# A new order of the steps of all five engines in a fused cross-attention and feed-forward kernel on one core

## Chip, cores, metric

The kernel runs on one NeuronCore of a Trainium2 chip (trn2). The metric is the device time of one execution in microseconds (us), median of the runs. The engines are TensorE (PE), VectorE (DVE), ScalarE (ACT), GpSimd (POOL) and SyncE (SP), which issues the DMA transfers. Each engine takes its instructions in order; between engines the program waits on semaphores.

## The reference

Eight batches of 512 rows with D = 512 go through cross-attention to 120 keys with 16 heads of 32, and then through a feed-forward block of width F = 2048 whose inputs are rounded to 8 bits and whose weights are rounded to three values. Cut to what matters:

```python
q = layernorm(x);  Q = q @ wq + bq;  K = ctx @ wk + bk;  V = ctx @ wv + bv
s = where(mask == 0, 1e-9, einsum('bhqd,bhkd->bhqk', Q, K) / sqrt(32))
x = x + (softmax(s) @ V) @ wo + bo
def bitlinear(x, w, b):                     # act_quant: round to 127 / max|x|; weight_quant: to -1, 0, 1
    return einsum('bsd,fd->bsf', act_quant(rmsnorm(x)), weight_quant(w)) + b
h = gelu(bitlinear(layernorm(x), w1, b1))
x = x + bitlinear(h, w2, b2)
```

## The kernel before

The 4096 rows are 32 tiles of 128 rows, numbered k = 0 to 31, four to a batch. A tile passes through a chain of steps, each a small helper that waits on semaphores, issues a few instructions on one engine and counts a semaphore up:

- layernorm by batch: SP `load_x` (L362, one 1 MB load of a batch), DVE `ln1_stats` (L1491), POOL `ln1_apply` (L2117), PE `turn_xn` (L535, transposes; the fourth of a batch lets SP load the next batch), ACT and DVE evacuate a high and a low part;
- attention: PE `project_q` (L528 in the helper `product3`, twelve matmuls: high and low parts), `project_ctx` (L560), `scores` (L581); DVE `softmax_max` (L1505, L1508), ACT `exps` (L1089), DVE `invert_sums` (L1513), POOL `normalize` (L2161), PE `turn_probs` (L591), ACT `evac_probs` (L1061), PE `attend` (L603), DVE `oT_low` (L1470), PE `project_out` (L528 again), DVE `residual` (L1518). `normalize`, `turn_probs` and `exps` go by quarter tiles, n = 4k to 4k + 3;
- first rounding: DVE `ln2_stats`, `ln2_scales` (L1524 to L1541), POOL `round_x` (L2129, L2134), then SP `turn_x(k)` (L328), a DMA transpose of the rounded tile q_x into `q_xT`. It waits for `round_x(k)` and for PE's use of an older buffer;
- feed-forward: PE `ffn_up(k, c)` for four chunks c (L632; chunk 0 waits for `q_xT`), DVE `evac_up` (L1554), ACT `gelu` (L1096), `square_h` (L1130), DVE `h_scale` (L1562), POOL `round_h` (L2172, L2177), SP `turn_h(k)` (L337), a DMA transpose of q_h into `q_hT` four times as large as that of q_x, PE `ffn_down(k, half)` for two halves (L655; the first waits for `q_hT`), POOL `h_factor` (L2195 to L2204) and `add_b2` (L2156), DVE `evac_down` (L1574), SP `store(k)` (L354). `load_residual(k)` (L323) brings the tile of x that the residual needs into one of six buffers and waits until the store of tile k - 6 has landed. ACT needs a table load when it changes between exponentials and gelu.

What sets the order is written out by hand: for each engine one list of calls in its block function (SP from about L369, PE from about L690, ACT from about L1156, DVE from about L1646, POOL from about L2217). Each list has a first part (the weights are loaded, transposed and rounded, the pipeline fills), `for a in range(2, 6)`, and a last part. One pass of the loop is one batch: four tiles in each step, several tiles deep, so that `scores(4a)`, `project_out(4a - 2)`, `ffn_up(4a - 4, 2)` and `ffn_down(4a - 5, 0)` stand near each other. SP's list in the loop begins with `store(4a - 6)`; all its transfers go through one queue in the order of issue:

```python
turn_x(4 * a - 2)
turn_h(4 * a - 4)
load_x(a + 2)
```

For the last tiles some steps go to other buffers: near the end `ffn_up` also writes banks that belonged to attention (`ps_s`, `ps_t`; DVE evacuates into `wk_s`, `wv_s`), the last tile is rounded in halves, and SP's `turn_last` brings the halves of it to PE.

Of the kernel before, what the change touches and what calls it, by code (L numbers as in the profile page):

```python
# [27 lines left out]
def xattn_bitffn_kernel(nc, x, ctx_in, mask, wq, bq, wk, bk, wv, bv, wo, bo, w1, b1, w2, b2, out):  # L28
# [104 lines left out]
    with ExitStack() as stack:  # L133
# [170 lines left out]
        def _(sp):  # L304
# [86 lines left out]
            load_piece(6)  # L391
            load_piece(5)
            load_residual(0)
            load_residual(1)
            load_piece(7)
            load_x(2)
            load_residual(2)
            load_residual(3)
            load_mask(1)
            load_ctx(2)  # L400
            load_residual(4)
            turn_x(0)
            load_residual(5)
            turn_x(1)
# [3 lines left out]
            store(0)  # L408
            turn_x(3)
            turn_h(1)  # L410
            load_mask(2)
            load_residual(6)
            turn_h(2)
            load_ctx(3)
            store(1)
            turn_x(4)
            load_residual(7)
            turn_h(3)

            for a in range(2, 6):  # L420
                store(4 * a - 6)
                turn_x(4 * a - 3)
                load_residual(4 * a)
                turn_x(4 * a - 2)
                turn_h(4 * a - 4)
                load_x(a + 2)
                store(4 * a - 5)
                store(4 * a - 4)
                turn_x(4 * a - 1)
                turn_h(4 * a - 3)  # L430
# [8 lines left out]
                turn_h(4 * a - 1)  # L439

            store(18)
            turn_x(21)
            load_residual(24)
            turn_h(20)
            store(19)
            turn_x(22)
            load_residual(25)
            turn_h(21)
            store(20)
            turn_x(23)  # L450
            load_mask(7)
            turn_h(22)
            turn_x(24)
            store(21)
            load_residual(26)
# [4 lines left out]
            load_residual(27)  # L460
            store(23)
            turn_h(24)
            load_residual(28)
# [28 lines left out]
        def _(pe):  # L492
# [230 lines left out]
            turn_piece(2, (2, 3))  # L723
            project_ctx(1, "k", wk_s)
            turn_xn(1, 0)
            scores(1)
            turn_probs(1)
            turn_piece(3, (0, 1))
            turn_piece(3, (2, 3))
            turn_probs(2)  # L730
            turn_xn(1, 1)
            turn_probs(3)
            project_ctx(1, "v", wv_s)
            turn_xn(1, 2)
            total_weights(1)
# [3 lines left out]
            scores(2)  # L739
            turn_keys(1)  # L740
            turn_probs(5)
            project_q(1, 0)
            turn_piece(4, (0, 1))
            turn_probs(6)
# [10 lines left out]
            scores(3)  # L755
            turn_piece(6, (2, 3))
            turn_probs(9)
            project_out(1)
            turn_piece(7, (0, 1))
            turn_probs(10)  # L760
            turn_piece(7, (2, 3))
            project_q(1, 3)
            turn_probs(11)
            turn_ctx(2)
            ffn_up(0, 0)
            turn_probs(12)
            attend(2)
            ffn_up(0, 1)
# [7 lines left out]
            turn_xn(2, 1)  # L776
            turn_probs(15)
            project_ctx(2, "k", wk_s)
            turn_probs(16)
            ffn_up(1, 0)  # L780
            attend(3)
            ffn_up(1, 1)
# [12 lines left out]
            ffn_up(2, 0)  # L795
            attend(4)
            ffn_up(2, 1)
            turn_probs(21)
            ffn_down(0, 0)
            ffn_down(0, 1)  # L800
            ffn_up(2, 2)
            project_q(2, 0)
# [1676 lines left out]
```

## Time and profile before

| | before |
|---|---|
| runs, us | 682.7 to 685.37, median 683.64 |
| profiled execution, span, us | 683.2 |
| PE busy, us | 641.6 |
| DVE, ACT, POOL busy, us | 576.9, 526.5, 514.7 |
| bytes moved by DMA | 65.38 MB |

The span of the profiled execution is 0.4 us under the median of the runs; it stands for the profiled execution's own time. Busy times add up the instructions of one engine, so that one engine's idle time is the span less its busy time. The window 0:242 holds the first part, 242:500 lies within the four passes of the loop, and the rest is the last part.

### The profile page before, as it was taken

How to read it: one execution, taken by the hardware profiler on the slowest of the kernel's cores; microseconds unless marked ns; L12 is line 12 of the kernel's file. 1: busy time of each engine (PE TensorE's matmuls, PEld its weight loads, DVE VectorE, ACT ScalarE, POOL GpSimd, SP SyncE). 2: the span in 40 equal slices, each digit the busy share in tenths (PEclk: the TensorE clock that was granted, in tenths of full speed). 3: DMA queues.
4: the chain of work that ended last, by engine and by line, in shares of the span. 5: the costliest groups of instructions: out<-in, count | busy, mean ns of one | idle time of the engine just before them, and what ended most of it. 6: DMA issues, size and time to landing. Idle time of an engine off the chain costs nothing.

```text
span 683.2 us, 13949 instructions
## 1 busy us (share of the span) xinstructions
PE 641.6 (94%) x4793; PEld 421.4 (62%) x4856; DVE 576.9 (84%) x1055; ACT 526.5 (77%) x1460; POOL 514.7 (75%) x653
## 2 busy tenths in 40 slices
PE   7989999888999999999999999999999999899987
PEld 6755876555666666666666666656666656555533
DVE  5687879888799988998799988999789889999894
ACT  2378668937988777877988778877988679998764
POOL 3196995588787699776977699776967676889975
PEclk9899999999999999999999999999999999999999
DMA  8980320133234333143334343153232330344336
GB/s 290 384 337 32 109 54 9 40 86 79 67 71 116 89 97 71 31 120 87 66 70 116 85 100 70 24 125 84 71 71 71 70 70 9 82 85 91 76 74 152
DMA packets 109285, 65.38 MB, mean 96 GB/s; under 512 B 90855, under 2 KB 90855, under 8 KB 108575
## 3 DMA queue, kind: packets, MB, share of 16 engines
q1 hardware_dynamic: 108159, 64.49, 36.3%
q8 instruction: 39, 0.64, 0.4%
q14 instruction: 31, 0.25, 0.1%
q10 hardware_dynamic: 1056, 0.00, 0.1%
HBM read 35.12 MB, written 8.39 MB: 64 GB/s over the span
## 4 chain that ended last, share of the span: by engine, by line
PE 49%; ACT 13%; POOL 12%; DVE 11%; DMA 7%; issue 5%; SPq 2%; POOLq 0%; DVEq 0%; ACTq 0%
PE ps_a L528 12%; PE ps_z L632 8%; PE ps_y L655 8%; PE ps_a L560 5%; ACT prob L1089 4%; PE ps_t L591 4%; DMA q_xT<-q_x 3%; PE ps_a L603 3%; POOL hid L2172 3%; PE ps_s L581 3%; POOL prob L2161 3%; POOL q_h L2177 3%; DMA xn<-in_x_dram 2%; DVE hs L1562 2%; DMA out_dram<-x 2%
## 5 line engine op out<-in xcount | busy, mean ns | idle before, releaser
L1089 ACT ACTIVATE prob<-ps_s,nmax 128x120 f32<-128x120 f32 x512 | 179.2, 380 | 42.8 <-DVE nmax L1508 38.6
L2161 POOL TENSOR_TENSOR prob<-prob,pinv 128x480 f32<-128x480 f32 x128 | 127.6, 1006 | 62.5 <-DVE pinv L1513 62.0
L632 PE MATMUL ps_z<-w1T,q_xT 128*128 128x512 bf16 x426 | 113.2, 379 | 11.9 <-DMA q_xT<-q_x 5.3
L1089 ACT ACTIVATION_READ_ACCUMULATOR prob<-ps_s,nmax 128x1 f32 x512 | 115.3, 225 | 0.0
L655 PE MATMUL ps_y<-w2T,q_hT 128*128 128x512 bf16 x439 | 105.0, 380 | 2.2 <-DMA q_hT<-q_h 1.8
L1505 DVE COPY_PREDICATED_SCALAR ps_s<-hidden_key,masked_c 128x480 f32 x128 | 90.5, 707 | 7.6 <-PE ps_s L581 7.3
L1554 DVE SCALAR_TENSOR_TENSOR hid<-ps_z,y_deq,b_row 128x512 f32<-128x512 f32 x116 | 85.7, 739 | 10.9 <-PE ps_z L632 9.0
L1061 ACT COPY probT<-ps_t 120x512 f32<-120x512 f32 x128 | 77.2, 603 | 18.6 <-PE ps_t L591 13.7
L1508 DVE TENSOR_REDUCE nmax<-ps_s 128x4 f32<-128x480 f32 x128 | 84.1, 657 | 4.4
L591 PE MATMUL ps_t<-ident,prob 128*120 128x128 f32 x512 | 78.3, 276 | 4.2 <-POOL prob L2161 2.7
L591 PEld LDWEIGHTS ps_t<-ident,prob 128*120 128x120 f32 x512 | 60.9, 138 | 27.6 <-issue 6.0
L632 PEld LDWEIGHTS ps_z<-w1T,q_xT 128*128 128x128 bf16 x476 | 42.9, 98 | 56.5 <-issue 15.3
L655 PEld LDWEIGHTS ps_y<-w2T,q_hT 128*128 128x128 bf16 x448 | 41.7, 98 | 52.9 <-issue 8.2
L2172 POOL TENSOR_SCALAR hid<-hid,hs 128x2048 f32<-128x2048 f32 x30 | 59.5, 1984 | 17.1 <-ACT q_h L1130 8.6
L1562 DVE TENSOR_REDUCE hs<-hid 128x1 f32<-128x2048 f32 x30 | 68.2, 2274 | 2.6 <-ACT hid L1096 2.6
L1096 ACT ACTIVATE hid<-hid 128x2048 f32<-128x2048 f32 x30 | 57.4, 1914 | 2.2 <-DVE hid L1554 1.9
L2124 POOL TENSOR_TENSOR x<-x,bo_row 128x512 f32<-128x512 f32 x32 | 41.2, 1288 | 20.9 <-DMA x<-in_x_dram 20.7
L528 PE MATMUL ps_a<-wo_h,oT_h 128*128 128x512 f32 x128 | 54.7, 428 | 1.5 <-DVE oT_l L1470 0.9
L2177 POOL TENSOR_SCALAR q_h<-hid 128x2048 bf16<-128x2048 f32 x28 | 53.8, 1921 | 2.4
L1130 ACT ACTIVATE q_h<-hid 128x2048 bf16<-128x2048 f32 x28 | 54.4, 1942 | 0.0
L528 PE MATMUL ps_a<-wo_l,oT_h 128*128 128x512 f32 x128 | 50.6, 395 | 0.0
L528 PE MATMUL ps_a<-wo_h,oT_l 128*128 128x512 f32 x128 | 50.5, 395 | 0.0
(193 smaller groups left out, 1377.0 us busy)
## 6 DMA issues: line engine op xcount, KB each, us to landing
x<-in_x_dram SPq DMA_DIRECT2D x32, 256.0 KB, 3.0
out_dram<-x SPq DMA_DIRECT2D x32, 256.0 KB, 2.7
xn<-in_x_dram SPq DMA_DIRECT2D x7, 1024.0 KB, 6.4
hid<-in_L_ffn_w_dram SPq DMA_DIRECT2D x4, 1024.0 KB, 10.2
w2T<-in_L_ffn_w_dram SPq DMA_DIRECT2D x2, 1024.0 KB, 12.5
ctx_k<-in_ctx_dram SPq DMA_DIRECT2D x8, 240.0 KB, 3.0
ctx_k<-in_mask_Bx1xSxS_ik_dram SPq DMA_DIRECT2D x7, 240.0 KB, 3.6
xn<-in_x_dram SPq DMA_DIRECT2D x4, 256.0 KB, 4.8
```

Source lines behind the costliest of these rows:

```text
L528: last = nc.tensor.matmul(bank, w, m, start=(k == 0 and i == 0), stop=(k == KD - 1 and i == 2))
L591: last = nc.tensor.transpose(ps_t[0:S2, g * P:(g + 1) * P], prob[:, n % 3, g * S2:(g + 1) * S2], ident[:])
L632: last = nc.tensor.matmul(bank[:], q_xT[:, k % 3, i], w1T[:, i, c * CH:(c + 1) * CH], start=(i == 0), stop=(i == KD - 1))
L655: last = nc.tensor.matmul(y_bank(k)[:], turned_h(k)[:, f], w2T[:, f], start=(f == 0), stop=(f == KF - 1))
L1061: nc.scalar.copy(probT[0:S2, i], ps_t[0:S2, :].rearrange("p (g q) -> p g q", g=G)).then_inc(s["p_evac"], 1)
L1089: last = nc.scalar.activation(prob[:, n % 3, g * S2:(g + 1) * S2], ps_s[n % HG][:, g * S2:(g + 1) * S2], ACT.Exp, bias=nmax[:, n % 4, g:g ...
L1505: v.copy_predicated(sc, hidden_key[:, k // T % 2, k % T].unsqueeze(1).to_broadcast([P, G, S2]), masked_c[:].unsqueeze(2).to_broadcast([P, ...
L1508: v.tensor_reduce(out=nmax[:, n % 4], in_=sc, op=ALU.max, axis=AX_X, negate=True).then_inc(s["sc_max"], 1)
L1554: v.scalar_tensor_tensor(hidden(k)[:, c * CH:(c + 1) * CH], z_bank(FC * k + c)[:], y_deq[:, k % 8:k % 8 + 1], b1_row[:, c * CH:(c + 1) * C ...
L1562: v.tensor_reduce(out=hs[:, 3, t:t + 1], in_=hidden(k), op=ALU.max, axis=AX_X, apply_absolute_value=True).then_inc(s["h_abs"], 1)
L2161: gp.tensor_tensor(pr, pr, pinv[:, n % 4].unsqueeze(2).to_broadcast([P, HG, S2]), ALU.mult).then_inc(s["prob_ready"], 1)
L2172: gp.tensor_scalar(magic(k), hidden(k), hs[:, 5, t:t + 1], MAGIC, ALU.mult, ALU.add).then_inc(s["h_magic"], 1)
```

## The change

Every engine's list gets a new order, in the first part, in the loop and in the last part. The same calls stand in each list before and after, with the same arguments; no helper, buffer, semaphore or operation changes. The diff has some 1,850 lines; its core follows. SP, loop and end:

```diff
             for a in range(2, 6):
+                turn_x(4 * a - 3)
                 store(4 * a - 6)
-                turn_x(4 * a - 3)
+                store(4 * a - 5)
+                load_residual(4 * a + 1)
+                turn_x(4 * a - 2)
+                load_x(a + 2)
                 load_residual(4 * a)
-                turn_x(4 * a - 2)
                 turn_h(4 * a - 4)
-                load_x(a + 2)
-                store(4 * a - 5)
                 store(4 * a - 4)
                 turn_x(4 * a - 1)
+                load_residual(4 * a + 2)
+                load_mask(a + 1)
                 turn_h(4 * a - 3)
-                load_mask(a + 1)
-                load_residual(4 * a + 1)
                 load_ctx(a + 2)
-                load_residual(4 * a + 2)
+                turn_x(4 * a)
                 turn_h(4 * a - 2)
                 store(4 * a - 3)
                 load_residual(4 * a + 3)
-                turn_x(4 * a)
                 turn_h(4 * a - 1)
...
-            store(26)
             turn_h(29)
             turn_h(30)
             turn_last(0)
+            turn_last(1)
+            store(26)
             store(29)
-            turn_last(1)
```

PE, first part, loop and last part:

```diff
             scores(5)
             turn_probs(17)
-            ffn_up(1, 2)
+            project_out(3)
             turn_xn(2, 2)
             turn_probs(18)
+            ffn_up(1, 2)
             turn_probs(19)
+            turn_xn(2, 3)
             ffn_up(1, 3)
             turn_probs(20)
-            project_out(3)
-            turn_xn(2, 3)
-            scores(6)
             project_ctx(2, "v", wv_s)
             ffn_up(2, 0)
+            scores(6)
             attend(4)
...
                 project_ctx(a + 1, "k", wk_s)
-                turn_probs(16 * a - 1)
+                ffn_up(4 * a - 3, 1)
+                turn_probs(16 * a)
                 ffn_down(4 * a - 5, 0)
-                turn_probs(16 * a)
-                ffn_up(4 * a - 3, 1)
                 attend(4 * a - 1)
...
             ffn_up(30, 1)
-            ffn_down(27, 0)
+            ffn_down(26, 1)
             ffn_up(30, 2)
             ffn_up(30, 3)
-            ffn_down(27, 1)
+            ffn_down(27, 0)
             ffn_up(31, 0)
             ffn_up(31, 1)
             ffn_up(31, 2)
+            ffn_down(27, 1)
             ffn_up(31, 3)
```

ACT, last part (in the first part, not shown, the new order has two more changes between exponentials and gelu; elsewhere as many as before):

```diff
             square_h(28)
+            gelu(29)
             round_h(28)
-            gelu(29)
             square_h(29)
             gelu(30)
+            square_h(30)
             round_h(29)
             gelu_last(0)
+            round_h(30)
             gelu_last(1)
-            round_h(30)
-            square_h(30)
```

DVE, loop and last part:

```diff
                 evac_down(4 * a - 6)
+                invert_sums(16 * a - 1)
+                evac_up(4 * a - 4, 2)
                 oT_low(4 * a - 2)
-                evac_up(4 * a - 4, 2)
                 softmax_max(16 * a)
+                softmax_max(16 * a + 1)
+                xT_low(a + 1, 0)
                 evac_up(4 * a - 4, 3)
-                xT_low(a + 1, 0)
-                softmax_max(16 * a + 1)
-                invert_sums(16 * a - 1)
                 residual(4 * a - 2)
...
             evac_up(28, 2)
-            evac_down(26)
             ln2_stats(30)
             evac_up(28, 3)
             ln2_scales(30)
+            oT_low(31)
             evac_up(29, 0)
-            oT_low(31)
+            evac_up(29, 1)
             h_scale(28)
-            evac_up(29, 1)
+            residual(31)
             evac_up(29, 2)
-            residual(31)
             evac_up(29, 3)
             ln2_stats(31)
+            evac_up(30, 0)
             ln2_scales(31)
-            evac_up(30, 0)
+            evac_down(26)
```

POOL, loop and last part:

```diff
+                round_x(4 * a)
+                round_h(4 * a - 2)
+                normalize(16 * a + 11)
                 add_bo(4 * a + 1)
-                h_factor(4 * a - 3)
-                normalize(16 * a + 8)
-                normalize(16 * a + 9)
-                ln1_factors(a + 2, 0, 4, 3 * a + 9)
-                round_h(4 * a - 2)
-                normalize(16 * a + 10)
-                normalize(16 * a + 11)
-                round_x(4 * a)
-                add_b2(4 * a)
                 y_factor(4 * a)
...
             normalize(125)
-            h_factor(26)
             normalize(126)
-            round_x(29)
             add_b2(27)
             normalize(127)
             y_factor(29)
+            round_x(29)
             round_h(27)
+            y_factor(30)
             round_x(30)
-            add_b2(28)
             add_bo(31)
             round_h(28)
-            y_factor(30)
+            h_factor(26)
             round_x(31)
             y_factor(31)
-            add_b2(29)
+            h_factor(27)
             round_h(29)
-            h_factor(27)
             round_h(30)
```

## Rows read from the trace of the kernel before

**Rows 1.** The page, part 1: busy time, share of the span and instructions of each engine.

```profile
PE 641.6 (94%) x4793; PEld 421.4 (62%) x4856; DVE 576.9 (84%) x1055; ACT 526.5 (77%) x1460; POOL 514.7 (75%) x653
```

**Rows 2.** Windows: stretch and its length, busy time of each engine, PE's granted clock, DMA share.

```profile
118.00:170.00 52.00, 43.94 (x367) 28.19 (x369) 44.31 (x80) 35.47 (x108) 36.47 (x45) 1.00 0.27 64
...
242.00:500.00 258.00, 252.62 (x1939) 166.11 (x1964) 224.79 (x421) 211.60 (x599) 207.92 (x269) 1.00 0.35 82
...
560.00:665.00 105.00, 94.28 (x715) 56.62 (x727) 95.53 (x173) 87.34 (x218) 85.21 (x113) 0.99 0.31 71
```

**Rows 3.** Waits of PE in 118:170: us in total, times, longest.

```profile
PE ps_a L528 <- DVE oT_l L1470: 2.0, 1, 2.0
PE ps_z L632 <- DMA q_xT<-q_x: 1.7, 1, 1.7
PE ps_t L591 <- ACT probT L1061: 1.4, 2, 1.2
PE ps_s L581 <- ACT prob L1089: 1.1, 1, 1.1
PE ps_t L591 <- POOL prob L2161: 1.0, 2, 0.7
```

**Rows 4.** Waits of PE in the loop, 242:500.

```profile
PE ps_z L632 <- DMA q_xT<-q_x: 3.5, 5, 1.2
```

**Rows 5.** Chain of waits in one pass of the loop: start, us, what.

```profile
287.05 2.79 PE ps_a L528 x12
...
295.45 1.29 PE ps_y L655 x6
...
312.83 0.02 issue
312.85 1.28 ACT L1089
314.13 0.01 issue
...
322.96 2.99 SPq L337
...
326.00 2.48 DMA out_dram<-x
...
328.92 2.69 DMA q_xT<-q_x
```

**Rows 6.** DMA issues: line, count, KB each, median us to landing.

```profile
xn<-in_x_dram SPq DMA_DIRECT2D x7, 1024.0 KB, 6.4
...
q_xT<-q_x SPq DMA_TRANSPOSE x32, 2.6
q_hT<-q_h SPq DMA_TRANSPOSE x29, 4.3
```

**Rows 7.** Chain of waits, first part, around 133 us.

```profile
132.81 0.38 SPq L362
...
133.24 5.66 DMA q_xT<-q_x
```

**Rows 8.** Chain of waits, last part.

```profile
632.70 0.20 POOL hs L2195
...
633.95 0.31 POOL h_deq L2204
...
640.65 1.99 POOL hid L2172
...
645.56 0.68 DVE oT_l L1470
...
679.91 0.75 DVE x L1574
```

**Rows 9.** Timeline of PE near the end; in brackets the idle time before.

```profile
662.78 0.92 PE L632 MATMUL ps_s<-w1T,q_xT 128*128 128x512 bf16 x2 [2.05 <-DVE wv_s L1554]
```

**Rows 10.** Windows of 4 us near the end.

```profile
664.00:668.00 4.00, 4.00 (x14) 1.56 (x14) 3.45 (x5) 3.10 (x3) 3.40 (x8) 0.71 0.69 131
```

More of the change, by code:

```diff
@@ L459, in _ @@
             store(22)
-            load_residual(27)
+            load_residual(28)
+            turn_h(24)
             store(23)
-            turn_h(24)
-            load_residual(28)
             load_residual(29)
@@ L754, in _ @@
             project_q(1, 2)
[L755 removed]
             turn_piece(6, (2, 3))
             turn_probs(9)
+            scores(3)
             project_out(1)
+            turn_probs(10)
             turn_piece(7, (0, 1))
[L760 removed]
+            project_q(1, 3)
             turn_piece(7, (2, 3))
[L762 removed]
             turn_probs(11)
[L764 removed]
             ffn_up(0, 0)
@@ L818, in _ @@
             project_q(2, 2)
+            ffn_up(3, 3)
             turn_probs(26)
-            ffn_up(3, 3)
             project_out(5)
+            ffn_up(4, 0)
+            turn_probs(27)
             turn_ctx(3)
-            turn_probs(27)
-            ffn_up(4, 0)
             project_q(2, 3)
-            ffn_down(2, 0)
+            ffn_up(4, 1)
             turn_probs(28)
             attend(6)
-            ffn_up(4, 1)
+            ffn_down(2, 0)
             ffn_down(2, 1)
@@ L990, in _ @@
             turn_probs(118)
-            ffn_down(24, 1)
+            project_out(28)
             ffn_up(27, 0)
             turn_probs(119)
-            project_out(28)
+            ffn_down(24, 1)
             ffn_up(27, 1)
+            attend(29)
             turn_probs(120)
-            attend(29)
+            ffn_up(27, 2)
             ffn_down(25, 0)
-            ffn_up(27, 2)
-            scores(31)
             turn_probs(121)
             ffn_down(25, 1)
+            scores(31)
             turn_probs(122)
@@ L1010, in _ @@
             ffn_up(28, 1)
+            project_out(30)
+            turn_probs(125)
             ffn_down(26, 0)
-            turn_probs(125)
-            project_out(30)
+            turn_probs(126)
             ffn_up(28, 2)
-            turn_probs(126)
-            ffn_down(26, 1)
+            ffn_up(28, 3)
             turn_probs(127)
-            ffn_up(28, 3)
             attend(31)
@@ L1751, in _ @@
             xT_low(2, 0)
-            residual(2)
+            softmax_max(19)
+            evac_up(1, 0)
             ln2_stats(2)
             invert_sums(17)
-            softmax_max(18)
+            h_scale(0)
             ln2_scales(2)
-            softmax_max(19)
-            evac_up(1, 0)
+            oT_low(3)
+            invert_sums(18)
+            softmax_max(20)
+            evac_up(1, 1)
+            invert_sums(19)
             xT_low(2, 1)
-            invert_sums(18)
-            invert_sums(19)
@@ L1762, in _ @@
-            evac_up(1, 1)
-            softmax_max(20)
+            softmax_max(21)
+            invert_sums(20)
+            xT_low(2, 2)
             evac_up(1, 2)
-            softmax_max(21)
+            residual(3)
             softmax_max(22)
-            invert_sums(20)
-            oT_low(3)
-            xT_low(2, 2)
+            evac_up(1, 3)
             softmax_max(23)
-            h_scale(0)
+            add_bv(2)
+            xT_low(2, 3)
             invert_sums(21)
-            residual(3)
@@ L2025, in _ @@
             invert_sums(118)
+            oT_low(28)
             h_scale(25)
@@ L2030, in _ @@
             softmax_max(121)
-            oT_low(28)
+            softmax_max(122)
+            softmax_max(123)
+            evac_up(27, 0)
             invert_sums(120)
-            softmax_max(122)
+            residual(28)
+            evac_down(24)
             invert_sums(121)
-            evac_down(24)
-            evac_up(27, 0)
-            softmax_max(123)
-            residual(28)
+            evac_up(27, 1)
+            ln2_stats(28)
+            ln2_scales(28)
             invert_sums(122)
-            ln2_stats(28)
-            evac_up(27, 1)
             h_scale(26)
             invert_sums(123)
-            ln2_scales(28)
+            evac_up(27, 2)
             oT_low(29)
-            evac_up(27, 2)
             softmax_max(124)
@@ L2374, in _ @@
             y_factor(23)
+            round_h(21)
+            h_factor(21)
             normalize(103)
-            h_factor(21)
-            add_b2(23)
             add_bo(25)
```

826 lines of the change are left out of this document (418 added, 408 removed).

## The prediction

> **What bounds the kernel now.** I first read the page. TensorE (PE) is busy for 641.6 of 683.2 us [rows 1], so the idle time that a new order could fill is 41.6 us at most; no operation goes away, so the kernel can't fall below about 642 us. Second, the windows by stage [rows 2]: the reader should take the difference of the first two numbers in each line. PE lacks 8.1 us in 118:170, only 5.4 us in the four passes of the loop (242:500) and 10.7 us in 560:665. Third, the waits of PE in the first two of these windows [rows 3, 4], which say for whom it idled; in the loop nearly all is one wait, 3.5 us in five times, of `ffn_up` for the transposed `q_xT`. Last, the chain of waits, for the loop [rows 5] and for the end [rows 8], says what comes just before such a gap.
>
> **The change, part by part.** All of it is order. In each stage I ask what fills a gap of PE, and which step now stands ahead of one that PE waits for.
>
> *First part.* PE waits between 118 and 170 for `turn_probs` 1.4 (ACT) and 1.0 (POOL), for `scores` 1.1, for `ffn_up(2,0)` 1.7 and for `project_q(2,2)` 2.0 us [rows 3]. The new list puts `project_out(3)` earlier, right behind `turn_probs(17)`, and `turn_xn(2,3)` ahead of `ffn_up(1,3)`. One product of this kind is 12 matmuls of 2.79 us together [rows 5]; with the `turn_xn` it can cover most of the three waits for probabilities, 1.4 + 1.0 + 1.1 = 3.5 us. `turn_x(2)` stays behind the 1 MB `load_x(3)`, but that load is released by `turn_xn(2,3)`, which comes earlier: I count 0.5 of its 1.7 us. The 2.0 us for `oT_low(5)` on DVE stay. Sum −4.0; bounds 0 and −5.9 (all of the rows but the 2.0 us, with the small remainder of the window).
>
> ACT pays for it: its new list alternates two more times between exponentials and gelu, each time with a table load of 1.28 us [rows 5], together 2.6 us. ACT is idle for 52 − 35.5 = 16.5 us in this window [rows 2], so I cost it at nothing; without that cover it is +2.6. Around the load in the loop's chain the rows leave 0.02 us ahead of it and 0.01 us behind it [rows 5].
> The Trainium skill, page "ScalarE: Activation LUTs", section "What ACT_TABLE_LOAD costs", counts about 1.38 us of drain beside the load, 2.66 us in all; by it, and with ACT on the path, the two switches would cost an estimated 5.3 us and the total would be about 684 us. The row shows no such drain, so I don't take it.
>
> *Loop, what is gained.* The chain before the gap at `ffn_up(4a,0)` is SP with `turn_h(10)`, then the landing of the store of tile 9 and, 2.69 us long, `turn_x(12)`, for whose end PE waits [rows 5]. (`load_residual(15)` stands behind that store for its buffer, and `turn_x(12)` behind `load_residual(15)`.) The new SP list has `turn_x(4a)` ahead of `turn_h(4a-2)`, and POOL rounds its input before `round_h(4a-2)`. `turn_x(12)` then no longer stands behind an issue of 2.99 us and a landing of 2.48 us, and can come some 5 us sooner; the whole 3.5 us [rows 4] go. The `turn_h(4a-2)` behind it comes later by one issue; `ffn_down(4a-2,0)`, which needs it, stands two steps behind `ffn_up(4a,0)` and is covered by `project_q`. −3.5 (0 to −3.5).
>
> *Loop, what is paid.* In the old list `turn_h(4a-4)` is issued ahead of `load_x(a+2)`; in the new one the 1 MB load and `load_residual(4a)` stand ahead of it. The load is released when PE ends `turn_xn(a+1,3)`, at 287.05 in this pass, where the row of the next product begins, and `ffn_down(4a-4,0)`, which needs the transposed `q_hT`, started at 295.45 [rows 5]. The new list has the same PE work between these two, so the transpose is wanted 8.4 us after the release. No row of before shows a `turn_h` behind a `load_x`. The near rows: `load_x` takes 6.4 us to land, a transpose of q_h 4.3 and one of q_x 2.6 [rows 6]. In the first part a `turn_x` was issued 0.43 us behind a `load_x` and took 5.66 us [rows 7], 3.1 more than its kind: it landed just behind the load, not beside it. A q_h transpose is four times as large, so (4.3 − 2.6) / 3 = 0.57 us for each 128 x 512 and 2.3 us for four, if only its data, and not its start, comes behind the load. I estimate that it lands at 0.2 (issue) + 6.4 + 0.9 (the residual's 256 KB: a quarter of the load's 6.4 would be 1.6, of which I take about half, since a landing has a fixed part too) + 2.3 = 9.8 us after the release, 1.4 us late. Bounds: 0, if the transfers mix; 0.2 + 6.4 + 0.5 + 4.3 = 11.4, or 3.0 us late, if nothing of the transpose overlaps the load. I take 1.4, by the `turn_x` behind the load, which is the nearest row; in four passes +5.6 (0 to +12.0).
>
> *Loop, the rest.* DVE's list groups the softmax maxima and residuals earlier and so brings several `evac_up` and `h_scale` later. DVE is busy for 224.8 of 258 us and POOL for 207.9 [rows 2], some 10 and 15 us free in a pass of 77 us; I expect small waits of PE in the shadow of the late `q_hT`, and cost them at nothing; without that shadow, two waits of half a microsecond a pass, +4. Loop in all: −3.5 + 5.6 = +2.1.
>
> *Last part.* POOL is on the chain up to `round_h(27)`, which starts at 640.65; `h_factor(26)`, from 632.70 to 634.26, stands in it [rows 8] and is moved behind `round_h(28)`, off this chain: −1.6. Then DVE is on the chain; it loses `oT_low(31)`, 0.68 us, which goes ahead of `evac_up(29,0)`, and gains `evac_down(26)`, 0.75 us by the last of its kind [rows 8]: +0.1. At 662.78 PE has idled 2.05 us for the `evac_up` into `wv_s` [rows 9], and thereafter the granted clock is 0.71 in a stretch of 4 us [rows 10], that is, PE ran at the lower level (1.2 of 2.4 GHz) for part of it; 4 x 0.29 = 1.2 us of work at full clock are missing. The new list puts `ffn_down(27,1)`, eight matmuls, into this idle time, just ahead of `ffn_up(31,3)`. The chain to the end runs through the slow matmuls, so I count 1.0 (0 to −1.2). Sum −1.6 + 0.1 − 1.0 = −2.5; bounds +0.8 (`evac_down(26)` paid in full and nothing gained) and −5.4 (half of PE's 10.7 us filled).
>
> **Sum.** −4.0 + 2.1 − 2.5 = −4.4 against the profiled execution's 683.2, hence 678.8 us; the median of the runs, 683.64, is 0.4 above that execution, so about 679.
>
> **Rivals.**
> A, slower: `turn_h(4a-4)` lands a full 4.3 us behind `load_x`, PE loses 3.0 us a pass, 12.0 − 3.5 = +8.5 in the loop, and in-order waits halve the 6.5 us gained elsewhere: 683.6 + 8.5 − 3.25 = 689. For it: the 3.1 us that the load added to a transpose [rows 7]. Against: that transpose hid its own start under the load. From about 2.5 us a pass on it decides (4 x 2.5 − 3.5 − 3.25 = +3.25).
> The Trainium skill, page "DMA: Bandwidth & Descriptors", section "Queues, rings and completion order", says that a DMA engine consumes the descriptors of a ring in ring order. The row of 5.66 us agrees.
> B, no change: the loop as forecast, +2.1, but every gap that PE fills comes back a step later, because DVE and POOL, in order too, bring an `evac_up` or a normalized probability later by as much; the first and the last part gain 1 us each: 683.7. For it: DVE is at 87% in the loop [rows 2], and many of its steps move. Against: the waits of rows 3 and 9 have PE work ready to fill them.
> C, faster by more: the transpose runs beside the load, the loop gives −3.5 and the sum is −10: 673.6. For it: the DMA engines are busy for a third of the loop only, 0.35 [rows 2]. Against: again the row of 5.66 us.
> That the change doesn't do what it says is excluded: SP's and PE's lists differ just where these gaps lie.
>
> **How the numbers follow.** A measurement can tell 0.5%, 3.4 us, from no change. The forecast, 0.33, and C, 0.17, lie below 680.2, so faster 0.50; B 0.28; A 0.22. The range, 670 to 690, leaves out the end where all bounds fall together on the good side (−5.9 − 3.5 − 5.4, 669) and on the bad one (12.0 + 0.8, 696). The likeliest case by itself gives 675 to 680.
>
> **What would show it.** In the new profile: the wait of `ffn_up` for `q_xT` in the loop under 1 us; a new wait of `ffn_down` (L655) for `q_hT` there, four times about 1.4 us; 118:170 with PE idle for 4 us instead of 8; `round_h(27)` on POOL about 1.6 us earlier against the end; no stretch of granted clock near 0.7 before the last tile's `ffn_down`. I am wrong if the wait for `q_hT` is over 2.5 us a pass or absent, or if waits for `evac_up` cost more than 1 us a pass.

## The result, and the profile after

The changed kernel takes 688.98 us (median of 6 runs, 686.99 to 692.18) against 684.9 us before on the same chips (median of 6): ratio 1.008, interval 1.0058 to 1.0102. By that ratio it is 0.8% slower, about 5.5 us; the two medians alone are 4.1 us apart. The profiled execution has a span (first to last instruction) of 685.2 us and a time of 686.99, the shortest of the six; the device time is 1.8 us over the span in each of them, so the profile of before, 683.2, belongs to a time of about 685, not to 683.6 as I had set it.

The first part of the page, and the three windows that answer to [rows 2]:

```profile
PE 640.4 (93%) x4856; PEld 417.6 (61%) x4856; DVE 573.3 (84%) x1055; ACT 533.9 (78%) x1462; POOL 514.9 (75%) x653
```

```profile
118.00:170.00 52.00, 49.72 (x406) 32.95 (x404) 45.21 (x87) 41.87 (x117) 38.80 (x49) 1.00 0.27 65
...
242.00:500.00 258.00, 248.20 (x1881) 160.90 (x1875) 220.78 (x409) 211.82 (x584) 203.39 (x260) 1.00 0.33 80
...
560.00:665.00 105.00, 98.07 (x747) 59.07 (x746) 98.96 (x181) 91.33 (x229) 88.28 (x115) 1.00 0.32 71
```

PE's busy time is unchanged. PE now lacks 2.3 us in 118:170 (8.1 before), 9.8 us in the loop (5.4 before) and 6.9 us in 560:665 (10.7 before): two of three stages went the way that was forecast, and the loop went the other way. The waits of PE in 118:170, against [rows 3]:

```profile
PE ps_z L632 <- DMA q_xT<-q_x: 1.5, 1, 1.5
PE ps_y L655 <- DMA q_hT<-q_h: 0.5, 1, 0.5
PE ps_s L581 <- ACT prob L1089: 0.3, 1, 0.3
```

Of the three waits for probabilities, 3.5 us before, 0.3 us is left, at `scores`; the one for `oT_low` is gone. ACT's two more table loads (ACT has 1462 instructions, 1460 before) delay nobody here: PE's waits for ACT fell from 2.5 to 0.3 us. The waits in the loop, against [rows 4]:

```profile
PE ps_t L591 <- POOL prob L2161: 5.3, 4, 1.3
PE ps_y L655 <- DMA q_hT<-q_h: 3.0, 3, 1.4
PE ps_a L528 <- DVE x L1518: 1.5, 4, 0.4
```

The wait for `q_xT` is gone, as forecast. In its place stand three others, 9.8 us in all: `turn_probs` for POOL's `normalize` (four times 1.3), `ffn_down` for `q_hT`, and `project_q`, which waits for DVE's `residual`. The chain of waits in one pass (start, us, what) says what comes before the first and the third:

```profile
231.10 1.23 POOL x L2156
...
234.91 1.41 POOL x L2156
...
241.71 1.24 POOL x L2156
...
244.47 1.26 POOL x L2156
245.73 0.68 POOL yw L2129
...
247.12 1.97 POOL hid L2172
...
249.18 1.90 POOL q_h L2177
251.08 0.95 POOL prob L2161
252.03 1.24 POOL x L2124
...
253.29 0.70 DVE x L1518
...
254.03 3.07 PE ps_a L528 x12
```

From 231 to 253 us all is POOL, without a gap. Four of its rows are L2156, `add_b2`, 5.1 us. Three of them, 3.9 us, the new list has moved here from earlier in the pass; the fourth, `add_b2(4a)`, stood behind `round_x(4a)` and now stands ahead of it, and so do the two `ln1_apply` (3.1 us, not shown). Then come `round_x(8)` (245.73) and `round_h(6)` (247.12, 249.18), and only then the one `normalize` of 1 us (251.08) that `turn_probs(43)` needs, though DVE's `invert_sums(43)`, which it waits for, had ended at 241.6 us. `add_bo(9)` (252.03) is behind it too, and DVE's `residual(9)` and PE's `project_q` wait for that. `turn_probs(16a+11)` stands right ahead of `ffn_up(4a,0)` on PE, so this wait sits where the old one was.

The other new wait, in the same view 40 us later:

```profile
285.81 0.49 SPq L362
...
286.36 0.50 SPq L323
...
286.96 7.93 DMA q_hT<-q_h
...
295.02 1.89 PE ps_y L655 x8
```

`load_x(5)` is issued at 285.81, `load_residual(12)` at 286.36, `turn_h(8)` at 286.96, and that one lands 7.93 us later; PE's `ffn_down(8,0)` starts at 295.02. At the end of the kernel the chain is POOL's again:

```profile
668.00 2.46 POOL x L2156 x2
...
670.55 0.52 POOL hs L2195
...
672.94 1.13 POOL qT L2183
...
679.42 2.46 POOL x L2156 x2
...
681.90 0.75 DVE x L1574
```

`add_b2(28)` and `add_b2(29)` (668.00) and `h_factor(30)` (670.55) run ahead of `round_last` (672.94, 668.93 before), and `add_b2(30)`, `add_b2(31)` (679.42) stand behind `h_factor(31)`; the last `evac_down` starts at 681.90, where it started at 679.91 before [rows 8].

### The profile page after: what moved, and what is told of

Its sections match the earlier page's. It is cut to its first block, busy times and chain, and to the rows that moved or that the text cites. A ratio compares the mean times of both kernels' runs of the same rounds, so it can differ in the third digit from the quotient of the medians.

```text
span 685.2 us, 14018 instructions
## 1 busy us (share of the span) xinstructions
PE 640.4 (93%) x4856; PEld 417.6 (61%) x4856; DVE 573.3 (84%) x1055; ACT 533.9 (78%) x1462; POOL 514.9 (75%) x653
## 4 chain that ended last, share of the span: by engine, by line
POOL 39%; PE 36%; DMA 8%; issue 7%; DVE 6%; ACT 2%; SPq 1%; POOLq 0%; DVEq 0%; ACTq 0%
PE ps_y L655 8%; PE ps_a L528 8%; POOL prob L2161 7%; DMA q_hT<-q_h 6%; POOL hid L2172 5%; PE ps_z L632 5%; PE ps_a L560 5%; POOL x L2156 4%; POOL q_h L2177 4%; PE ps_t L591 3%; POOL xn L2117 3%; PE ps_a L603 2%; POOL x L2124 2%; PE ps_s L581 2%; POOL hs L2198 1%
## 5 line engine op out<-in xcount | busy, mean ns | idle before, releaser
L632 PE MATMUL ps_z<-w1T,q_xT 128*128 128x512 bf16 x476 | 122.7, 380 | 6.6 <-DVE hid L1554 3.4
L1089 ACT ACTIVATION_READ_ACCUMULATOR prob<-ps_s,nmax 128x1 f32 x512 | 111.9, 219 | 0.0
L1554 DVE SCALAR_TENSOR_TENSOR hid<-ps_z,y_deq,b_row 128x512 f32<-128x512 f32 x116 | 85.8, 739 | 20.7 <-PE ps_z L632 18.3
L591 PEld LDWEIGHTS ps_t<-ident,prob 128*120 128x120 f32 x512 | 60.2, 137 | 32.8 <-issue 14.1
L632 PEld LDWEIGHTS ps_z<-w1T,q_xT 128*128 128x128 bf16 x476 | 42.5, 98 | 57.2 <-issue 15.5
L2124 POOL TENSOR_TENSOR x<-x,bo_row 128x512 f32<-128x512 f32 x32 | 41.1, 1285 | 19.2 <-DMA x<-in_x_dram 19.1
```

The costliest lines, as they stand in the source:

```text
L591: last = nc.tensor.transpose(ps_t[0:S2, g * P:(g + 1) * P], prob[:, n % 3, g * S2:(g + 1) * S2], ident[:])
L632: last = nc.tensor.matmul(bank[:], q_xT[:, k % 3, i], w1T[:, i, c * CH:(c + 1) * CH], start=(i == 0), stop=(i == KD - 1))
L1089: last = nc.scalar.activation(prob[:, n % 3, g * S2:(g + 1) * S2], ps_s[n % HG][:, g * S2:(g + 1) * S2], ACT.Exp, bias=nmax[:, n % 4, g:g ...
L1554: v.scalar_tensor_tensor(hidden(k)[:, c * CH:(c + 1) * CH], z_bank(FC * k + c)[:], y_deq[:, k % 8:k % 8 + 1], b1_row[:, c * CH:(c + 1) * C ...
```

## The experiments

The kernels below are splices of the two lists or move single calls; nothing is left out of the computation. Ratios are to the kernel before on the same chip. One table for the four rounds, from the ends of PE's steps in each trace (us; "opening" is `scores(0)` to `turn_probs(0)`, "fill" `turn_probs(0)` to `ffn_down(2,1)`, "seam" from there to `ffn_up(8,0)`, "three passes" to `ffn_up(20,0)`, "last" to `ffn_up(28,3)`, "end" to the end of the span):

| kernel | ratio (interval) | opening | fill | seam | three passes | last | end |
|---|---|---|---|---|---|---|---|
| before | 1 | 13.0 | 137.1 | 69.0 | 230.9 | 155.2 | 41.5 |
| after | 1.008 (1.0058 to 1.0102) | 13.5 | 132.2 | 72.5 | 236.8 | 150.3 | 44.5 |
| e1 first part only | 1.0052 (1.003 to 1.0075) | 17.4 | 131.1 | 73.9 | 231.3 | 155.1 | 41.5 |
| e2 loop only | 1.013 (1.0096 to 1.0164) | 12.8 | 137.3 | 71.2 | 237.3 | 155.8 | 41.1 |
| e3 last part only | 0.999 (0.9965 to 1.0014) | 13.4 | 136.4 | 68.8 | 231.3 | 149.6 | 47.5 |
| e4 no loop | 1.0045 (1.0018 to 1.0073) | 18.9 | 131.0 | 74.5 | 233.2 | 149.0 | 47.8 |
| e6 tail early | 1.0067 (1.0045 to 1.0089) | 14.5 | 131.5 | 74.5 | 236.6 | 150.2 | 46.1 |
| e8 add_b2 early | 1.0022 (0.9995 to 1.0049) | 17.6 | 131.1 | 70.6 | 233.8 | 150.1 | 44.4 |
| e9 first part mended | 0.9957 (0.9934 to 0.9981) | 15.5 | 131.1 | 70.8 | 233.0 | 155.3 | 41.5 |
| e13 turn_x early | 0.9946 (0.9927 to 0.9965) | 15.4 | 137.4 | 67.6 | 228.3 | 155.1 | 41.7 |
| e14 load_x ahead | 1.0047 (1.0029 to 1.0065) | 12.6 | 138.3 | 70.5 | 232.3 | 155.1 | 40.9 |
| e15 add_b2 late | 1.0053 (1.003 to 1.0076) | 12.7 | 137.5 | 69.5 | 233.4 | 155.3 | 41.1 |
| e16 best | 0.9869 (0.984 to 0.9897) | 15.9 | 131.2 | 69.6 | 228.6 | 149.7 | 43.7 |

The columns are of one traced execution each, the ratios of all runs. The time up to `scores(0)`, 32.5 to 36.6 us, is in no column. It and the opening vary with the granted clock (last section), so a ratio isn't the sum of its columns.

**First round: one part at a time.** Each kernel takes the whole new order of one part, on all engines, into the kernel before; the fourth takes the loop out of the changed kernel.

> The kernel before with the new order in the first part alone, all engines. Theory (each part acts by itself): in the profiles ffn_down(2,1), the last step of PE's first part, ended 5.5 us earlier after the change (181.15 against 186.65), and nothing in the old loop takes that back, so 4 to 6 us faster than before. Rival (a lead at the start of the loop is only borrowed, because POOL or DMA sets the loop's pace): the lead is gone by the first passes, 0 to 1.5 us faster.

Measured: 686.74 us, 1.0052, slower. Both theories fell. PE does save 6 us in the fill, but it pays 4.4 us ahead of it and 5 us behind it. The first price is in ACT's timeline and in PE's waits from 28 to 52 us:

```profile
36.27 1.90 ACT L1152 CAST wo_h<-x 128x2048 fp32r<-128x2048 f32 x1 [4.77 <-DMA x<-in_L_xattn_wo_dram]
38.08 0.59 ACT L1148 ACTIVATE w1T<-ps_z 128x512 bf16<-128x512 f32 x1
```

```profile
PE ps_z L678 <- ACT w1T L1148: 5.7, 2, 4.9
```

`round_wo` (36.27) waits 4.77 us for the load of wo, and the `evac_piece(0,0)` behind it (38.08), 0.6 us of work whose input was ready, waits along; PE then waits 4.9 us for it. Behind this idle stretch PE runs for part of 6 us at the lower of its two levels (1.2 of 2.4 GHz), by the granted clock of 0.72 in the window (the clock is the third number from the right; before it is 1.00 there):

```profile
38.00:44.00 6.00, 5.19 (x15) 3.30 (x16) 5.06 (x5) 3.90 (x19) 4.33 (x4) 0.72 0.91 343
```

So the 4.4 us are the wait and the slow matmuls behind it, less what PE waited for here before. The second price is in POOL's timeline:

```profile
190.64 1.27 POOL L2124 TENSOR_TENSOR x<-x,bo_row 128x512 f32<-128x512 f32 x1 [3.42 <-DMA x<-in_x_dram]
```

`add_bo(7)` waits 3.42 us for `load_residual(7)`, which the new list has behind `turn_h(3)`; everything behind it on POOL comes that much later.

> The kernel before with the new order in the loop alone. Theory: each of the four passes gets about 2 us longer (ffn_up(8,0) to ffn_up(20,0), three passes: 236.8 us after, 230.9 before), so 6 to 10 us slower than before, with waits of turn_probs for POOL and of ffn_down for q_hT in the loop. Rival (the loop lost time only because it gave a lead back): 0 to 3 us slower.

Measured: 691.84 us, 1.013, 9 us slower, as the theory had it, and with its waits (5.1 us for POOL, 3.5 for `q_hT`, 1.5 for `residual` in 242:500). The loop is where the change loses.

> The kernel before with the new order in the last part alone. Theory: from ffn_up(21,3) to ffn_up(31,3) the new order gained 6 us in the profiles, and the end gives 2 us back because POOL's round_last comes behind two add_b2 and h_factor(30), and add_b2(30), add_b2(31) behind h_factor(31): together 3 to 5 us faster than before. Rival (the gain in the last part was only the catching up of what the loop had lost): 0 to 2 us slower, the price of the end alone.

Measured: 681.68 us, 0.999: no difference. PE gains 5.6 us up to `ffn_up(28,3)` and loses 6 us behind it. Of that, 1.5 us lie behind PE's last step (the POOL chain shown above); much of the rest follows an idle stretch of PE. Timeline of PE (idle time before in brackets) and a window of 4 us:

```profile
644.38 1.02 PE L632 MATMUL ps_z<-w1T,q_xT 128*128 128x512 bf16 x4 [2.28 <-DMA q_xT<-q_x]
...
646.50 3.19 PE L655 MATMUL ps_y<-w2T,q_hT 128*128 128x512 bf16 x8
```

```profile
644.00:648.00 4.00, 3.62 (x12) 1.49 (x13) 3.48 (x8) 3.41 (x2) 1.84 (x6) 0.71 0.00 0
```

After 2.28 us of idleness for `q_xT` the granted clock falls to 0.71 (part of the stretch at 1.2 of 2.4 GHz), and `ffn_down(26,1)`, which the new list has put ahead of `ffn_up(30,2)`, takes 3.19 us instead of 1.89. It fills PE's time, but, as I read it, it delays a step that DVE's chain waits for; no run moves it alone.

> The changed kernel with the loop's old order on all engines. Theory (the parts add up): 7 to 11 us faster than before, 674 to 678 us if before reads 685. Rival (leads are borrowed): 0 to 3 us faster.

Measured: 685.45 us, 1.0045 (1.0018 to 1.0073). Neither theory had it: without the loop the rest is still slower, through the two prices of the first part and the end's. First and last part do add up: 0.5% (e1) and −0.1% (e3) make the 0.45% measured. The loop doesn't: with its 1.3% (e2) the three make 1.7%, and the changed kernel is 0.8% slower. The loop's order costs 9 us between the old parts and about 2.4 us between the new ones (1.008 against 1.0045, with intervals of 1.5 to 2 us either way). The seam shows part of it: e1 adds 4.9 us to it, e2 2.2, and both together 3.5.

**Second round: single steps of the changed kernel put back.**

```diff
-            round_wo()
             evac_piece(0, 0)
             exps(0)
+            round_wo()
```

> The changed kernel with one step of ACT's first part back in its old place: round_wo behind exps(0), not ahead of evac_piece(0, 0). Theory: round_wo waits for the 1 MB load of wo, which lands at 36 us, and evac_piece(0, 0) and with it PE's turn_piece(0, (2, 3)) wait behind it; that step ended 4.3 us after scores(0) or later in every profile with the new first part, and 2.9 to 3.8 us with the old one, with up to 7.9 against 3.8 where the opening ran at full clock. So 2 to 4 us faster than the changed kernel (689), about 686; turn_probs(0) at 46 to 49 us. Rival (the opening is set by the weight loads themselves and the step is covered): no change, 688 to 690.

Measured: 688.94 us, 1.0074 (1.0048 to 1.0101): no gain that its time can tell, so the rival's forecast; no trace of it is read. The traces with this step back (e9, e11, e12 and e16) have an opening of 14.1 to 16.2 us against 17.4 to 18.9 in e1, e4, e7 and e8, so 1 to 5 us seem to be saved there; but the opening also varies with the granted clock (with the old first part 12.6 to 12.8 us where the clock is 1.00 throughout, and 15.4 in e13, where its mean is 0.89). In the profile of the changed kernel itself PE came to this point late (`scores(0)` ended at 35.4 instead of 32.8), when the load of wo had nearly landed, and the cost was mostly hidden: its opening is 13.5 us, and 14.5 in e6, where `scores(0)` ended at 36.4.

```diff
             h_factor(29)
+            round_last()
             add_b2(28)
             add_b2(29)
             h_factor(30)
-            round_last()
+            add_b2(30)
             h_factor(31)
-            add_b2(30)
             add_b2(31)
```

> The changed kernel with two steps of POOL's last part back: round_last ahead of add_b2(28), and add_b2(30) ahead of h_factor(31). Theory: after the change round_last began at 672.9 instead of 668.9 and add_b2(31) ended at 681.9 instead of 677.2, and evac_down(31) waited for it; 2 to 2.6 us faster than the changed kernel, about 686.5. Rival (the end then waits for turn_last and ffn_down(31,1) as long): 0 to 0.8 us faster.

Measured: 689.06 us, 1.0067. The rival was nearer: 5.0 us from PE's last step to the end became 4.3. POOL had still the deferred `add_b2`, 1.25 us each, behind `round_last`; in e10, which has one of them earlier, these 4.3 us are 3.4, as before the change.

```diff
                 turn_x(4 * a - 2)
-                load_x(a + 2)
-                load_residual(4 * a)
                 turn_h(4 * a - 4)
+                load_x(a + 2)
+                load_residual(4 * a)
```

> The changed kernel with load_x(a + 2) and load_residual(4a) back behind turn_h(4a - 4) in SP's loop. Theory: the wait of ffn_down(4a-4,0) for q_hT, 0.8 to 1.7 us in each of four passes, goes: 3 to 5 us faster than the changed kernel, a pass of about 77.9 us instead of 78.9. Rival (POOL sets the pace of the loop): the wait turns up at turn_probs(16a+11) for POOL, 0 to 1.5 us faster in all, a pass stays at 78.6 or more.

Measured: 691.61 us, 1.0123 (1.0087 to 1.0159), slower still. Neither had it. The wait for `q_hT` was gone from the loop, but the residual came later with the load, and POOL's list has `add_bo(4a)` in the middle of its pass:

```profile
377.74 1.26 POOL L2124 TENSOR_TENSOR x<-x,bo_row 128x512 f32<-128x512 f32 x1 [8.62 <-DMA x<-in_x_dram]
```

POOL stood idle for 8.62 us for that residual (4.62 us in the same place of the changed kernel), ahead of the stretch in which it has no idle time, and PE's waits for POOL in the loop doubled to 10.6 us.

```diff
                 add_bo(4 * a - 1)
+                add_b2(4 * a - 3)
...
                 y_factor(4 * a - 2)
+                add_b2(4 * a - 2)
...
                 round_x(4 * a - 1)
+                add_b2(4 * a - 1)
...
                 h_factor(4 * a - 3)
-                add_b2(4 * a - 3)
...
                 normalize(16 * a + 8)
-                add_b2(4 * a - 2)
...
                 normalize(16 * a + 10)
-                add_b2(4 * a - 1)
                 ln1_apply((2, 3))
-                add_b2(4 * a)
...
                 add_bo(4 * a + 1)
+                add_b2(4 * a)
```

> The changed kernel with the four add_b2 of a pass on POOL back to about their old places, ahead of the stretch in which POOL has no idle time; the rest of POOL's loop stays new. Theory: the normalize that turn_probs(16a+11) waits for, and add_bo(4a+1) behind it, come up to 3.8 us earlier; the wait of 1.3 us and the 0.4 us of project_q behind residual(4a+1) go, 1.5 to 1.7 us a pass, 5 to 7 us in all, about 683. Rival (the new list only moved POOL's work and the load ahead of turn_h sets the pace): 0 to 2 us faster.

Measured: 685.68 us, 1.0022, so 0.6% better than the changed kernel by the ratios, about 4 us; a pass takes 77.9 instead of 78.9 us. Waits of PE in the loop:

```profile
PE ps_t L591 <- POOL prob L2161: 3.8, 6, 1.0
PE ps_y L655 <- DMA q_hT<-q_h: 0.4, 2, 0.2
```

The wait for `q_hT` shrank with it, from 3.0 to 0.4 us, though SP's list is that of the changed kernel. The wait at `turn_probs(16a+11)` is gone, and a new one for POOL, 1.0 us a pass, stands at `turn_probs(16a+1)`; a pass is still 1.0 us longer than before. The rival fell: POOL's order was the larger part. What else in it costs the rest was not tried.

**Third round: mended parts.** e9 is e1 with `round_wo` back as in e5, and on SP:

```diff
+            load_residual(7)
             turn_h(3)
-            load_residual(7)
```

e10 is e3 with one filler on PE, its `evac_down` on DVE and POOL's end put otherwise:

```diff
             ffn_up(30, 1)
-            ffn_down(26, 1)
             ffn_up(30, 2)
             ffn_up(30, 3)
+            ffn_down(26, 1)
...
-            evac_down(26)
             evac_up(30, 1)
             evac_up(30, 2)
             evac_up(30, 3)
             h_scale(29)
+            evac_down(26)
...
             h_factor(27)
+            add_b2(28)
             round_h(29)
             round_h(30)
             h_factor(28)
             h_factor(29)
-            add_b2(28)
             add_b2(29)
-            h_factor(30)
             round_last()
+            h_factor(30)
+            add_b2(30)
             h_factor(31)
-            add_b2(30)
             add_b2(31)
```

e11 is the changed kernel with the edits of e5, e8 and e10; e12 has the first part of e9, the old loop and the last part of e10.

> The kernel before with the new order in the first part alone (as in the first experiment), and two steps of it back: round_wo behind exps(0) on ACT, and load_residual(7) ahead of turn_h(3) on SP. Theory: with the first part new, POOL's add_bo(7) waited to 190.6 us for that residual, everything behind it on POOL came 3.4 us late, and PE lost its lead at ffn_up(5,0) and turn_probs(31); with both back the lead lasts: 3 to 6 us faster than before, ffn_down(2,1) to ffn_up(8,0) takes 69 to 71 us instead of 73.9, turn_probs(0) lies at 46 to 48 us. Rival (the lead of PE is given back at the next step of another engine in any case): within 2 us of before, 73 us or more.

Measured: 680.7 us, 0.9957, 3 us faster than before and, by the ratios, 6 us faster than e1. The seam takes 70.8 us instead of 73.9, and the wait for `evac_piece` is down to 1.2 us:

```profile
PE ps_z L678 <- ACT w1T L1148: 1.2, 2, 0.9
```

> The kernel before with the new order in the last part alone, and these steps of it put otherwise: add_b2(28) and add_b2(29) ahead of the stretch at the end in which POOL has no idle time, round_last ahead of h_factor(30), add_b2(30) ahead of h_factor(31); ffn_down(26,1) behind ffn_up(30,3) instead of ahead of ffn_up(30,2), with evac_down(26) behind h_scale(29). Theory: the new last part gains 5 us up to ffn_up(28,3) and loses 1.4 to 4.8 us behind it through a filler that stands ahead of a late step, and 1.5 us at the end through POOL's deferred add_b2; with these back 4 to 7 us faster than before. Rival (the chain of DVE and POOL behind ffn_up(28,3) sets the end anyway): 0 to 2 us faster.

Measured: 682.83 us, 0.9993 (0.9971 to 1.0014). POOL's end was mended (17.6 us from `ffn_up(31,3)` to the end of the span, 20.7 in e3), but my other edit made a wait of its own: `evac_down(26)` behind `h_scale(29)` kept `ffn_down(27,0)` waiting, and the clock fell again behind it. The waits of PE from 560 to 682, and the window behind this one:

```profile
PE ps_y L655 <- DVE x L1574: 3.6, 1, 3.6
```

```profile
656.00:660.00 4.00, 4.00 (x12) 1.51 (x11) 1.94 (x4) 2.23 (x3) 3.92 (x3) 0.57 0.11 22
```

> The changed kernel with round_wo behind exps(0), with the four add_b2 of the loop on POOL early, and with the last part put as in the run beside it. Theory: the mends add up, about 4 us from the loop and 3 to 5 us from the end, 679 to 682 us where before reads 684. Rival (what is gained in one part is given back in the next): no better than the run with add_b2 early alone, 684 to 687.

Measured: 682.8 us, 1.0012 (0.9992 to 1.0033): better than the changed kernel by 0.7%, and not yet better than before.

> New first part with its two steps back, old loop, new last part mended as in the runs beside it. Theory: the gains of the two add up, 7 to 12 us faster than before, 672 to 677. Rival: the lead of the first part is lost in the loop and only the last part's gain stays, 0 to 5 us faster.

Measured: 680.49 us, 0.9962 (0.9943 to 0.9981): the rival's figure, the first part's gain with none from the last part, for e10's reason.

**Fourth round: the loop's three pieces, each by itself in the kernel before.** e13, e14 and e15:

```diff
                 turn_h(4 * a - 2)
+                turn_x(4 * a)
                 store(4 * a - 3)
                 load_residual(4 * a + 3)
-                turn_x(4 * a)
```

```diff
+                load_x(a + 2)
                 turn_h(4 * a - 4)
-                load_x(a + 2)
```

```diff
                 h_factor(4 * a - 5)
-                add_b2(4 * a - 3)
...
                 y_factor(4 * a - 2)
-                add_b2(4 * a - 2)
...
                 round_x(4 * a - 1)
-                add_b2(4 * a - 1)
...
                 h_factor(4 * a - 3)
+                add_b2(4 * a - 3)
                 normalize(16 * a + 8)
+                add_b2(4 * a - 2)
...
                 normalize(16 * a + 10)
+                add_b2(4 * a - 1)
```

> The kernel before with turn_x(4a) directly behind turn_h(4a-2) in SP's loop, ahead of store(4a-3) and load_residual(4a+3); nothing else. Theory: the wait of ffn_up(4a,0) for q_xT, 1.2 us a pass, goes and nothing takes its place: 3 to 5 us faster than before, a pass of 75.8 us instead of 76.9. Rival (PE then waits for POOL or DVE at the same place): 0 to 1.5 us faster, the pass stays over 76.5.

Measured: 679.2 us, 0.9946: 3.7 us faster. The wait for `q_xT` has left the loop, and what remains is 0.9 us:

```profile
PE ps_z L632 <- issue: 0.5, 3, 0.2
PE ps_z L632 <- DVE hid L1554: 0.4, 1, 0.4
```

> The kernel before with load_x(a + 2) ahead of turn_h(4a - 4) in SP's loop; nothing else. Theory: turn_h lands 8 to 9 us after the load's release and ffn_down(4a-4,0) waits 0.3 to 1 us, 1 to 4 us slower than before. Rival A of the prediction (a full 4.3 us behind the load): a wait of 2 us and more a pass, 8 us slower or more. Rival (the work between covers it): no change within 1 us.

Measured: 686.22 us, 1.0047 (1.0029 to 1.0065): 3.2 us slower, within the theory's range. But in its trace the price is not paid every pass. The first pass, ahead of 242 us, waits 1.9 us for `q_hT`; the second waits longer at the old gap, `ffn_up(12,0)`, 1.9 us where it was 1.1; the other two are as before. PE's waits in 170:242, then in 242:500:

```profile
PE ps_y L655 <- DMA q_hT<-q_h: 1.9, 1, 1.9
```

```profile
PE ps_z L632 <- DMA q_xT<-q_x: 3.4, 4, 1.9
...
PE ps_y L655 <- DMA q_hT<-q_h: 0.4, 2, 0.2
```

> The kernel before with add_b2(4a-3), (4a-2) and (4a-1) moved behind h_factor(4a-3), normalize(16a+8) and normalize(16a+10) in POOL's loop, as late as the change has them; nothing else. Theory: POOL, idle earlier in the pass, has 3.8 us more to do just ahead of round_h(4a-2), normalize(16a+11) and round_x(4a), so ffn_up(4a,0) waits longer: 1 to 3 us a pass, 4 to 10 us slower than before. Rival (POOL has enough idle time there): within 1.5 us of before.

Measured: 685.73 us, 1.0053 (1.003 to 1.0076): 3.6 us slower, just under the theory's range. These are three of the pass's four `add_b2`. `ffn_up(4a,0)` waits up to 1.9 us where it waited 1.2, 4.7 us in all where it was 3.5. In the chain of waits ahead of the 1.9 us, POOL's late `add_b2` (312.62) stands ahead of `round_h(10)` (316.59), whose transpose, a store's landing and `turn_x(12)` follow; before, POOL waited there for ACT:

```profile
PE ps_z L632 <- DMA q_xT<-q_x: 4.7, 4, 1.9
```

e16 is e12 with e13's edit in the loop, and `evac_down(26)` one step earlier:

```diff
             evac_up(30, 3)
+            evac_down(26)
             h_scale(29)
-            evac_down(26)
```

> As the best version of the runs before (new first part with its two steps back, old loop, new last part mended), with evac_down(26) behind evac_up(30,3) instead of behind h_scale(29), and with turn_x(4a) early in the loop as in e13. Theory: ffn_down(27,0) no longer waits 3.6 us for evac_down(26), and the loop gains 1.2 us a pass: 7 to 11 us faster than before. Rival (the gains in loop and last part don't last): 2 to 4 us faster, as that version.

Measured: 673.57 us, 0.9869 (0.984 to 0.9897): 1.3% faster than before, the fastest of the kernels here. Its waits of PE in the loop:

```profile
PE ps_t L591 <- POOL prob L2161: 1.2, 1, 1.2
...
PE ps_z L632 <- DVE hid L1554: 0.4, 1, 0.4
```

## Why the prediction was wrong

The table tells where it went wrong. By the traced executions, the first part (opening and fill) gained 4.4 us (4.0 forecast), the loop (seam and three passes) lost 9.4 (2.1 forecast), and the last part (last and end) gained 1.9 (2.5 forecast); another 1.2 us came ahead of `scores(0)`. The 9.4 are not the loop's order alone: there the new first part by itself costs 5.3 us (e1), the new loop by itself 8.6 (e2). By its steps:

- *First part, −4.0.* The waits went as forecast, and more: the fill took 5 to 6 us less in every trace with the new first part, and even the 2.0 us for `oT_low(5)`, which I had left standing, are gone. (The bound −5.9 should read −6.1, 8.1 less 2.0.) What I missed lies outside 118:170. `round_wo` had been moved ahead of `evac_piece(0,0)`, and I gave it no term: 4.4 us in the opening, slow matmuls included (e1), though mostly hidden in the changed kernel. And `load_residual(7)` behind `turn_h(3)` cost 3 us with the old loop behind it (e1 against e9). So the first part alone is 0.5% slower, not faster; this is the smaller miss in the changed kernel.
- *Loop, what is gained, −3.5.* Right by itself: e13 gained 3.7 us. In the changed kernel it was not to be had, since POOL kept the step just ahead of `ffn_up(4a,0)` waiting as long.
- *Loop, what is paid, +5.6.* In the changed kernel place, mechanism and size were right. `turn_h(8)` landed 9.1 us after the load's release (9.8 forecast); PE waited 0.8 to 1.7 us for it in each of four passes, 4.7 us in all. The Trainium skill, page "DMA: Bandwidth & Descriptors", section "Queues, rings and completion order", has descriptors consumed in ring order; the 7.93 us agree with that, and the transpose was not held for its full 4.3 us behind the load. The load alone cost 3.2 us (e14), but only in the first two passes.
- *Loop, the rest, "cost at nothing".* **This is the step that failed.** I read POOL's 207.9 of 258 us as 15 free us a pass and looked at DVE's moves. But POOL's free time is not spread over the pass. It lies where POOL waits for DVE's `invert_sums` and, the longest single wait, for a residual; behind that wait 0.6 us is left up to `round_x(4a)`. Waits of POOL in 242:500 and its timeline, both of the kernel before:

```profile
POOL prob L2161 <- DVE pinv L1513: 15.8, 12, 3.2
POOL x L2124 <- DMA x<-in_x_dram: 12.9, 3, 4.5
```

```profile
311.56 1.33 POOL L2124 TENSOR_TENSOR x<-x,bo_row 128x512 f32<-128x512 f32 x1 [4.24 <-DMA x<-in_x_dram]
```

  The new list moves three `add_b2`, 3.9 us, from ahead of that wait to behind it, and the fourth and both `ln1_apply` ahead of `round_x(4a)`; so the 22 us without a gap. In the changed kernel this term is 6.8 us in the loop window, not 0: 5.3 for POOL at `turn_probs` and 1.5 for `residual` behind it. The three `add_b2` alone cost 3.6 us (e15), and taking the four back gains 4 us (e8). Loop in all: +2.1 forecast, about 9 measured (e2). The three pieces tried alone (e13, e14, e15) add up to +3.1 us only; the other 6 us lie in how they meet, as for the gain above, and in moves of POOL and DVE that were not tried alone, the `ln1_apply` among them.
- *Last part, −2.5.* In the changed kernel's trace nearly met: the wait for the `evac_up` into `wv_s` is 0.4 us instead of 2.05, and from 560 to 680 us the granted clock is 1.00. But e3 shows 0. The gain up to `ffn_up(28,3)` is 5 us, larger than I had it; the `add_b2` deferred to the end got no term (1.5 us behind PE's last step), and I did not see that `ffn_down(26,1)` now stands ahead of steps that DVE needs early. `round_h(27)` starts 44.4 us ahead of the end instead of 42.5, as forecast, but those 1.8 us did not come off the end.
- *Rival A* named 689 us, but by 3.0 us a pass for `q_hT`; about 1.2 was measured, so the figure is met by luck. *Rival B* has the mechanism: in-order POOL gives back what PE gains. Its place was POOL far more than DVE, and its price higher than the 4.5 us between it and the forecast.
- *The signs of being wrong* that I had named did not come: the wait for `q_hT` was neither absent nor over 2.5 us a pass, and the loop window has no wait for `evac_up`. The loss came through a wait that I had not listed.

What stays open: which of the moves not tried alone make up the rest of the loop's loss, and why two fifths of the last part's gain are still given back in e16 (43.7 us behind `ffn_up(28,3)` against 41.5).

## What to carry to other kernels

Price a reordering on every engine's list, and for each deferred step ask whether that engine still has idle time where the step lands; an average of free time over a loop says nothing about that. A filler on PE is good only behind the steps that another engine's chain waits for next. And in an in-order list a step that waits for a load (here `round_wo` or `add_bo`) must not stand ahead of short work that is ready.

## What the runs showed of the hardware

SP's issue of a transpose can itself be held up by what is queued ahead. In the changed kernel's SP timeline:

```profile
286.96 5.82 SPq L337 DMA_TRANSPOSE q_hT<-q_h  x1
```

In the six traces in which the 1 MB `load_x` stands ahead of `turn_h(4a-4)` (the changed kernel, e2, e6, e8, e11, e14), this instruction took 5.05 to 6.01 us on SP in each of the four passes; in the others 1.7 to 2.8, and no other transpose of q_h took over 3.6. In e14 no residual stands between, so the load alone is enough. SP's next steps waited with it.

Second, the granted clock differs between executions ahead of `scores(0)`, where PE's list is the same in all. Windows of the kernel before and of e1:

```profile
0.00:30.00 30.00, 25.02 (x115) 20.34 (x116) 17.35 (x23) 9.95 (x13) 5.29 (x15) 0.89 0.95 338
```

```profile
0.00:30.00 30.00, 26.46 (x132) 21.16 (x133) 17.90 (x27) 10.56 (x14) 6.78 (x16) 1.00 0.95 337
```

In four of the 17 traces read (before, after, e6, e10) the clock is 0.89 to 0.94 there, and `scores(0)` ended at 35.4 to 36.6 us; in the others it is 1.00, and `scores(0)` ended at 32.5 to 33.5. So the traces of the two kernels compared here both begin some 3 us late. Why the clock falls in some executions and not in others isn't shown.
